# An attention-and-experts kernel: one stack moved ahead, the routing steps dealt out anew, rotary rotations in fours, and scatters that wait for TensorE once a turn

## The reference

```python
def reference(x, Wq, Wk, Wv, Wo, bo, router_w, router_bias, wg, wu, wd, swg, swu, swd):
    xn = layernorm(x)
    # attention: 16 query heads of 16, one key/value head, window of 64 keys
    q, k, v = heads(xn @ Wq), xn @ Wk, xn @ Wv
    q, k = rope(q, dims=8), rope(k, dims=8)     # x1,x2 = dims 0:4, 4:8
    scores = q @ k.T * 16**-0.5 + window_mask   # 0 <= i - j < 64
    attention = (softmax(scores) @ v).merge_heads() @ Wo + bo
    # ffn: 64 experts, top 4 of softmax(logits), chosen by logits + bias
    logits = xn @ router_w
    idx = top_k(logits + router_bias, 4)
    gates = normalised softmax(logits)[idx]
    routed = sum over the 4: gate * (silu(xn @ wg[e]) * (xn @ wu[e])) @ wd[e]
    shared = sum over 2: (silu(xn @ swg) * (xn @ swu)) @ swd
    return x + attention + routed + shared
```

## Time and profile before

| | us |
|---|---|
| median of three runs | 364.16 (363.85 to 364.17) |
| the profiled execution, its own time | 364.63 |
| its span | 363.3 |
| busy: PE, PEld | 337.3, 250.7 |
| busy: DVE, ACT, POOL | 250.7, 181.7, 251.7 |
| turns 0 to 15 | 30.4 to about 150 |

### The profile page before, as it was taken

One profiled execution on the slowest core, in us unless ns is written; L12 is line 12 of the kernel. 1 busy time (PEld: TensorE's weight loads), 2 busy tenths in 40 slices (PEclk: granted clock), 3 DMA queues, 4 the chain that ended last, 5 costly groups with the idle time before them and its releaser, 6 DMA issues.

```text
span 363.3 us, 8649 instructions
## 1 busy us (share of the span) xinstructions
PE 337.3 (93%) x2711; PEld 250.7 (69%) x2711; DVE 250.7 (69%) x721; ACT 181.7 (50%) x343; POOL 251.7 (69%) x506
## 2 busy tenths in 40 slices
PE   6978779899999999999999999999999999999982
PEld 3776546666665665589999999999975456655572
DVE  4778788988999997556456545444476376668686
ACT  2677378797688786454555555555442101110100
POOL 6467388878778777425666667778884777777774
PEclk9989899999999999999999999999999999999998
DMA  8950235645496567689988764587974344444444
GB/s 253 230 148 1 63 104 153 199 146 163 140 254 168 163 200 214 199 249 255 351 289 259 246 197 155 189 255 253 328 261 154 98 120 130 131 125 122 130 130 130
DMA packets 73036, 66.81 MB, mean 184 GB/s; under 512 B 9053, under 2 KB 68701, under 8 KB 72993
## 3 DMA queue, kind: packets, MB, share of 16 engines
q1 hardware_dynamic: 66433, 49.30, 45.8%
q0 software_dynamic: 6144, 16.79, 14.8%
q10 hardware_dynamic: 416, 0.18, 0.3%
HBM read 36.78 MB, written 29.23 MB: 182 GB/s over the span
## 4 chain that ended last, share of the span: by engine, by line
PE 70%; DVE 17%; issue 5%; ACT 5%; DMA 1%; POOL 1%; SPq 1%; DVEq 0%; POOLq 0%; ACTq 0%
PE bank L665 17%; PE bank L604 15%; PE bank L690 10%; PE bank L624 7%; PE bank L639 5%; PE bank L418 4%; DVE xall L1102 3%; PE bank L406 2%; PE bank L555 2%; PE bank L487 2%; DVE xall L1339 2%; PE bank L530 1%; ACT xall L861 1%; DVE xall L1096 1%; DMA wdn<-edges 1%
## 5 line engine op out<-in xcount | busy, mean ns | idle before, releaser
L1517 POOL DMA_INDIRECT xs_d<-spare,slot_i x64 | 63.7, 996 | 24.9 <-issue 7.3
L1609 POOL DMA_INDIRECT wall<-y_d,y_row x64 | 62.7, 980 | 24.9 <-issue 18.9
L665 PE MATMUL bank<-xall,spare 128*128 x508 | 63.8, 278 | 0.0
L1293 DVE TENSOR_TENSOR spare<-bank,spare 64x512 f32<-64x512 f32 (+1 forms) x64 | 44.1, 690 | 28.2 <-ACT spare L910 27.3
L665 PEld LDWEIGHTS bank<-xall,spare 128*128 128x128 f32 x508 | 59.4, 192 | 2.1
L1544 POOL COPY spare<-wall 128x256 f32 x127 | 49.1, 408 | 17.0 <-PE bank L665 9.1
L604 PE MATMUL bank<-xnT,xall 128*128 128x512 f32 x128 | 57.3, 594 | 0.0
L923 ACT ACTIVATE spare<-bank 128x512 f32<-128x512 f32 (+1 forms) x62 | 33.7, 593 | 28.0 <-PE bank L690 18.6
L861 ACT ACTIVATE xall<-bank 98x1024 bf16<-98x1024 bf16 x32 | 32.9, 1027 | 19.3 <-PE bank L437 17.7
L604 PEld LDWEIGHTS bank<-xnT,xall 128*128 128x128 f32 x128 | 24.1, 190 | 25.2 <-issue 24.4
L886 ACT ACTIVATE xall<-bank 128x512 f32<-128x512 f32 x16 | 9.5, 597 | 59.6 <-PE bank L604 59.6
(11 more groups left out here) (174 smaller groups left out, 635.3 us busy)
## 6 DMA issues: line engine op xcount, KB each, us to landing
y_d<-spare SPq DMA_DIRECT2D x31, 512.0 KB, 4.1
wall<-in_wg SPq DMA_DIRECT2D x16, 256.0 KB, 3.4
wall<-in_wu SPq DMA_DIRECT2D x16, 256.0 KB, 4.3
wdn<-in_wd SPq DMA_DIRECT2D x16, 256.0 KB, 4.5
spare<-xs_d SPq DMA_DIRECT2D x32, 128.0 KB, 3.5
small<-xs_d SPq DMA_DIRECT2D x32, 128.0 KB, 3.6
wall<-in_x SPq DMA_DIRECT2D x4, 512.0 KB, 5.4
base_d<-spare SPq DMA_DIRECT2D x16, 128.0 KB
```

The source lines that it names most:

```text
L665: ins = pe.matmul(up_bank_of(G)[:, j * P:(j + 1) * P], wcur[i % NW][:, c * 2 * F:(c + 1) * 2 * F], x_half[c][:, bass.ds(o, P)], start=c == ...
L1293: ins = dve.tensor_tensor(hT[G % 2][half, 0:n], up_bank_of(G)[F:P, 0:n], sg[0:F, 0:n], ALU.mult)
L1517: pool.indirect_dma_start(out=xs_d, out_offset=bass.IndirectOffsetOnAxis(ap=slot_i[:, T, k:k + 1], axis=0), in_=x_n[b][:, t, :], in_offset ...
L1609: pool.indirect_dma_start(out=yk[:, T, k, :], out_offset=None, in_=of, in_offset=bass.IndirectOffsetOnAxis(ap=y_row[:, T, k:k + 1], axis=0 ...
```

## The change

TensorE's and ScalarE's `stack(1, 1)` come ahead of the totals of the routing instead of behind them. In turn 0 VectorE does `near(1)` before the routing step instead of after it. One `yield` more splits the ranks (both halves' additions in one step) from the two steps with `max` and `slot_i`. `route_at` has four places: two as before, the third now before `place(T)`, the fourth between `place(T)` and `near(T+1)`. `cast(3, 0)` moves from ScalarE's turn 1 to the end of turn 0. `expert_row()` moves ahead of `place(T)` on TensorE. GpSimd rotates tiles 4 to 7 with four instructions on four tiles at once, between the scatters of turn 0 and of turn 1, tiles 8 to 11 with four instructions between the scatters of turn 5, and tiles 12 to 15 in turn 9; `roped` counts tiles up to 3 and then fours. One rotation buffer moves into a free part of another region, and the cosines and sines are stored twice. The scatters of a turn wait only for `maxima(T, 0)`, and `SCATTERED_AT` deals out 4 or 5 of them to each turn.

```diff
--- before.py
+++ after.py
@@ -57,7 +57,7 @@
     inv = np.exp(-np.log(np.float32(ROPE_BASE)) * (np.arange(0, 2 * ROT, 2).astype(np.float32) / np.float32(2 * ROT))).astype(np.float32)
     theta = (pos[:, None] * inv[None, :]).astype(np.float32)
     part = np.arange(P)
-    rows = lambda a: np.ascontiguousarray(a.reshape(TPB, P, ROT).transpose(1, 0, 2).reshape(P, TPB * ROT))
+    rows = lambda a: np.ascontiguousarray(np.repeat(a.reshape(TPB, P, 1, ROT), 2, 2).transpose(1, 0, 2, 3).reshape(P, TPB * 2 * ROT))
     f32 = {
         "ident": np.eye(P),
         "cos": rows(np.cos(theta)),
@@ -214,7 +214,7 @@
     wproj = ar.take(NC * NPROJ).rearrange("p (c n) -> p c n", c=NC)
     qrow = [ar.take(H * (SROWS + MROWS), bf16).rearrange("p (h n) -> p h n", h=H) for _ in range(2)]
     qtok = [r[:, :, 0:SROWS].rearrange("p h (c d) -> p h c d", d=HD) for r in qrow]
-    rope = [ar.take(H * 2 * ROT).rearrange("p (h i d) -> p h i d", h=H, i=2) for _ in range(2)]
+    rope = [r.take(TPB * H * 2 * ROT).rearrange("p (t h n) -> p t h n", t=TPB, h=H) for r in (early, ar)]
     rest = ar.take(H * HD).rearrange("p (h d) -> p h d", d=HD)
     SCORES_AT = ar.o // D
     NQ = 3
@@ -321,10 +321,12 @@
 
     FIRST = 10
 
-    ROUTE = ((1, 1, 1), (1, 0, 1))
-    route_at = lambda T: ROUTE[T] if T < len(ROUTE) else (0, 0, 2 - T % 2 if T < 12 else 1)
+    ROUTE = ((1, 1, 0, 1), (1, 1, 0, 0), (0, 0, 1, 1), (0, 0, 1, 0), (0, 0, 1, 1), (0, 0, 1, 0), (0, 0, 1, 1), (0, 0, 1, 0),
+             (0, 0, 1, 1), (0, 0, 0, 1), (0, 0, 1, 1), (0, 0, 1, 1))
+    route_at = lambda T: ROUTE[T] if T < len(ROUTE) else (0, 0, 0, 1)
     EXPERT_ROW, EXPONENTS, BIAS_AT = 13, 4, 18
-    SCATTERED_AT = lambda T: 6 if T in (NT - 4, NT - 3) else 4
+    SCATTERED_AT = lambda T: 5 if T in (2, 3, 4, 6, 7, 8) or T > 9 else 4
+    roped_with = lambda T: T + 1 if T < TPB else TPB + T // TPB
 
     NORM = ((0,), (1,), (2, 3))
 
@@ -725,13 +727,14 @@
             for t in late_tile(T, 2):
                 project(t)
             if T == 0:
+                stack(1, 1)
                 totals()
                 for i in range(2):
                     rank(i)
             if T:
                 scores(T - 1, 0, 0)
                 scores(T - 1, 0, 1)
-            if T + 1 < NT:
+            if 0 < T < NT - 1:
                 stack(T + 1, 1)
             if T > 1:
                 attention(T - 2)
@@ -740,6 +743,8 @@
                 scores(T - 1, 1, 1)
             for t in late_tile(T, 3):
                 project(t)
+            if T == EXPERT_ROW:
+                expert_row()
             place(T)
             if 0 < T < NT - 1:
                 weigh(T - 1, 0)
@@ -747,8 +752,6 @@
                 stack_k(T + 2)
             if 0 < T < NT - 1:
                 weigh(T - 1, 1)
-            if T == EXPERT_ROW:
-                expert_row()
             if 1 < T < NT - 1:
                 project_out(T - 2)
 
@@ -845,7 +848,7 @@
             if part == 0:
                 if T >= 2:
                     act.wait_ge(s["q_T"], 2 * (T - 2) + 2)
-                act.wait_ge(s["roped"], T + 1)
+                act.wait_ge(s["roped"], roped_with(T))
             else:
                 act.wait_ge(s["q_left"], 2 * T + 1)
             source = q if part == 0 else rest
@@ -965,7 +968,7 @@
         for T in range(NT):
             for t in late_tile(T, 0):
                 copy_q(t)
-            if T + 2 < NT:
+            if T + 2 < NT and T != 1:
                 cast(T + 2, 0)
             if T + 1 < NT:
                 stack(T + 1, 0)
@@ -975,6 +978,8 @@
                 cast(T + 2, 1)
             for t in late_tile(T, 2):
                 copy_q(t)
+            if T == 0:
+                stack(1, 1)
             if T:
                 scores(T - 1, 0, 0)
                 scores(T - 1, 0, 1)
@@ -985,9 +990,10 @@
                 scores(T - 1, 1, 1)
             for t in late_tile(T, 3):
                 copy_q(t)
-            if T + 1 < NT:
+            if 0 < T < NT - 1:
                 stack(T + 1, 1)
             if T == 0:
+                cast(3, 0)
                 act.wait_ge(s["c32"], 16)
                 act.activation(unread[:, :], ident[:, 0:1], ACT.Exp)
             if T == EXPONENTS:
@@ -1214,6 +1220,9 @@
                 dve.wait_ge(s["ranked"], i + 1)
                 dve.tensor_tensor(lifted[:, ts, :], bank[2 + i][:, :].rearrange("p (t e) -> p t e", e=E),
                                   starts[:, i, :].unsqueeze(1).to_broadcast([P, 8, E]), ALU.add).then_inc(s["rank_read"], 1)
+            yield
+            for i in range(2):
+                ts = slice(8 * i, 8 * i + 8)
                 dve.wait_ge(s["rank_read"], i + 1)
                 for t in range(8 * i, 8 * i + 8):
                     ins = dve.max(pos8[:, t, :], lifted[:, t, :])
@@ -1390,10 +1399,14 @@
                 next(route, None)
             if T + 2 < NT:
                 leave(T + 2, 1)
-            place(T)
             for _ in range(steps[2]):
                 next(route, None)
-            if T + 1 < NT:
+            place(T)
+            if T == 0:
+                near(1)
+            for _ in range(steps[3]):
+                next(route, None)
+            if 0 < T < NT - 1:
                 near(T + 1)
             if T:
                 output(T - 1)
@@ -1472,8 +1485,7 @@
             pool.wait_ge(s["kv_out"], b + 1)
             k = qk[:, ts, H, :]
             x1, x2 = k[:, :, 0:ROT], k[:, :, ROT:2 * ROT]
-            cs = k32["cos"].rearrange("p (t d) -> p t d", d=ROT)
-            sn = k32["sin"].rearrange("p (t d) -> p t d", d=ROT)
+            cs, sn = [k32[n].rearrange("p (t d) -> p t d", d=2 * ROT)[:, :, 0:ROT] for n in ("cos", "sin")]
             pool.tensor_tensor(krope[0], x1, cs, ALU.mult)
             pool.tensor_tensor(krope[1], x2, sn, ALU.mult)
             pool.tensor_tensor(krope[2], x1, sn, ALU.mult)
@@ -1490,21 +1502,23 @@
             prep(pool.tensor_tensor(krest[1], krest[0], parts[:, :, 1, :], ALU.subtract))
             pool.tensor_copy(parts[:, :, 2, :], krest[1]).then_inc(s["k_split"], 1)
 
-        def rotate(T):
-            t = T % TPB
-            pool.wait_ge(s["proj_q"], T + 1)
-            q = qk[:, T, 0:H, :]
-            x12 = q[:, :, 0:2 * ROT].rearrange("p h (i d) -> p h i d", i=2)
-            over = lambda v: v[:, t * ROT:(t + 1) * ROT].unsqueeze(1).unsqueeze(1).to_broadcast([P, H, 2, ROT])
-            if T:
-                pool.wait_ge(s["roped"], T)
-            pool.tensor_tensor(rope[0], x12, over(k32["cos"]), ALU.mult)
+        def rotate(lo, hi):
+            pool.wait_ge(s["proj_q"], hi)
+            q = qk[:, lo:hi, 0:H, :]
+            x12 = q[:, :, :, 0:2 * ROT]
+            n, t = hi - lo, lo % TPB
+            over = lambda v: v[:, 2 * ROT * t:2 * ROT * (t + n)].rearrange("p (t d) -> p t d", t=n).unsqueeze(2).to_broadcast([P, n, H, 2 * ROT])
+            a, b = [r[:, 0:n] for r in rope]
+            first, second = slice(0, ROT), slice(ROT, 2 * ROT)
+            if lo:
+                pool.wait_ge(s["roped"], roped_with(lo - 1))
+            pool.tensor_tensor(a, x12, over(k32["cos"]), ALU.mult)
             yield
-            prep(pool.tensor_tensor(rope[1], x12, over(k32["sin"]), ALU.mult))
+            prep(pool.tensor_tensor(b, x12, over(k32["sin"]), ALU.mult))
             yield
-            pool.tensor_tensor(x12[:, :, 0], rope[0][:, :, 0], rope[1][:, :, 1], ALU.subtract)
+            pool.tensor_tensor(x12[:, :, :, first], a[:, :, :, first], b[:, :, :, second], ALU.subtract)
             yield
-            pool.tensor_tensor(x12[:, :, 1], rope[0][:, :, 1], rope[1][:, :, 0], ALU.add).then_inc(s["roped"], 1)
+            pool.tensor_tensor(x12[:, :, :, second], a[:, :, :, second], b[:, :, :, first], ALU.add).then_inc(s["roped"], 1)
             yield
 
         def scatter():
@@ -1565,30 +1579,27 @@
                 find_down(G + 1)
 
         pool.wait_ge(s["c32"], 16)
-        def rotate_whole(T):
-            for _ in rotate(T):
+        def rotate_whole(lo, hi):
+            for _ in rotate(lo, hi):
                 pass
 
-        rotate_whole(0)
+        rotate_whole(0, 1)
         prepare_k(0)
-        rotate_whole(1)
+        rotate_whole(1, 2)
         prepare_k(1)
         prepare_k(2)
-        rotate_whole(2)
-        rotate_whole(3)
+        rotate_whole(2, 3)
+        rotate_whole(3, 4)
         prepare_k(3)
         slots = scatter()
         for T in range(NT):
 
-            pieces = rotate(T + TPB) if T < NT - TPB else iter(())
+            if T == 1:
+                rotate_whole(TPB, 2 * TPB)
+            pieces = rotate(T + 3, T + 3 + TPB) if T in (TPB + 1, 2 * TPB + 1) else iter(())
             for i in range(SCATTERED_AT(T)):
-                if T > 0:
-                    if i < 2:
-                        pool.wait_ge(s["by_query"], PER_T * T + 2 * i + 2)
-                    elif i == 2:
-                        pool.wait_ge(s["by_key"], PER_T * (T - 1) + 3)
-                    else:
```

(3 more changed lines are left out.)

## The result

The changed kernel takes 371.54 us (median of 4 runs, 370.05 to 372.79), the kernel before, run beside it, 364.17. The ratio is 1.0202, with a 95% interval of [1.0172, 1.0232]: slower by 1.7 to 2.3%. A second comparison on another occasion gives 369.45 for 364.14, ratio 1.0123 [1.0056, 1.019].

The account below looks back on a forecast made before the run. It took PE to bound the kernel (busy 93% of the span), with the change acting on turns 0 to 15. Terms +1.9, +2.0, +3.7 and -0.5 gave +7.1 on 364.63; less some for contention, it said 370.9, range 365.2 to 375.5.

Parts of the forecast that it names:

- the late rotation in turn 2: Turn 2: GpSimd rotates tiles 4 to 7 only by 54.1, so ScalarE's cast is late and the 4.3 us lead goes.
- turn 3 starts later: Start of turn 3: 61.4 against 60.52, 0.9 lost, plus 1.0 for the low clock; +1.9 us.
- steps ahead of `place`: Turns 3 to 11: routing steps moved ahead make PE wait for VectorE's `place`; +2.0 us, from -0.5 to +3.
- turns 5 and 9: Four-tile rotations between scatters end late, so ScalarE's cast is 1.45 and 2.25 us too late; +3.7 us.
- rest: Remaining turns: `expert_row` moved ahead removes PE's 0.48 us wait; -0.5 us.
- Turns 0 and 1: a gain: `near(1)` no longer stands behind the routing step; turn 1 at about 40.8, turn 2 at 48.9, 4.3 us ahead.
- Contention prolongs the steps: Alternative for the routing steps moved ahead of `place`: contention makes them longer, +3 us instead of +2.0.
- Each scatter no longer waits for TensorE gains nothing: Scatters end earlier, at about turn 13, but turns 12 to 15 run on PE; no gain by itself.
- the cheap rotations: Rival: four large rotation instructions take 2.0 us together and the clock holds in turn 3; sum +1.9, 366 us; chance 0.17.
- the faster case: Rival: the cast of tile 4 is not late, the first two turns' 4.3 us stay; -2.8, 361.4 us; chance 0.07.
- low clock more than priced: Rival: dear rotations add 2.7 us, or low clock behind turn 9's wait up to 1.7; 374 to 375 us; chance 0.16.

Follow-up runs that it names:

- 2b: Changed kernel with all three four-tile rotations ahead of the scatters of turns 0, 5 and 9; 363.0 us, 0.9949 of the kernel before (364.14).
- experiment 6: Changed kernel with four-tile rotations ahead of their turn's scatters and routing steps of turns 2 to 11 behind `place(T)`; 362.33 us, ratio 0.9957 to the kernel before.
- f3: Changed kernel, rotations ahead of the scatters of turns 0, 5 and 9, as single-tile instructions; 428.13 us, ratio 1.104 where the kernel before takes 389.55.
- second set: Four kernels (two of them the changed kernel with edits, one it unedited, one the kernel before with four-tile rotations) run where the kernel before takes 364.14 us.
- experiment 5: Kernel before with only the four-tile rotations of the change, its own waits, routing and scatters kept; 372.49 us, ratio 1.0213 to the kernel before.
- experiment 2: Changed kernel with all three four-tile rotations ahead of their turn's scatters, on a chip where the kernel before takes 391.34 us; 434.0 us, ratio 1.1143.

## Why the prediction was right, by its own steps

The time and the sign came out: 370.9 was said, 371.54 measured, and in the profiled execution +5.4 where the sum was +7.1. That the number is so near is in part luck. Against the profiled execution three terms are 1.1 to 1.2 us too high and one is 1.7 too low, and on the second occasion the same kernel took 369.45. The mechanism of the largest loss, the late rotation in turn 2, was right. The terms, against the turn starts of before and after:

| term | predicted | measured |
|---|---|---|
| turn 3 starts later | +1.9 | +0.84 |
| steps ahead of `place` (turns 3, 4, 6, 7, 8, 10, 11; the prediction has +0.2 for turn 5 in it) | +2.0 | +0.87 |
| turns 5 and 9 | +3.7 | +1.82, +3.53, together +5.35 |
| rest (turns 12 to 14, then to the end) | -0.5 | -0.92, -0.74 |

- **Turns 0 and 1: a gain, as said, and larger.** Turn 1 starts at 39.54 (40.8 said), turn 2 at 47.11 (48.9). 1.1 of it lies ahead of the turns: turn 0 starts at 29.26 instead of 30.39, as the granted clock is 1.00 from 20 to 23 where it was 0.50 from 20 to 23 before. In the second profiled execution of the changed kernel it is 0.71, 0.50 and 0.50 there and turn 0 starts at 30.00, so this differs from execution to execution and is no effect of the change. Turn 1 itself is 7.57 long (8.1 said). Which of the edits brings what in these two turns, no run takes apart.
- **Turn 2: the mechanism was right, shown by 2b, two sizes were off and cancelled.** `slot_i` was ready at 43.27, not 44.8, and the first scatter at 44.16. The four rotation instructions took 1.27, 1.26, 0.73 and 0.73, 3.96 from first start to last end, not 3.4: the slope of 1.7 ns an element read from the earlier trace rows was too low. The estimate of 3.9 from the Trainium skill (GPSIMD Engine Reference, section 3.1, Elementwise) was the better one; the trace, with 3.96, agrees with it. The cast began at 53.23 instead of 54.1, and the low clock took the 0.9 back: PE's `project`, 1.03 at full clock, took 1.91. Turn 3 starts at 61.36; the chain of waits alone was said to give 61.4, and I had added 1.0 for the low clock on top.
- **Steps ahead of place: the wait is there, its price was not.** PE waits 1.48 before line 445 in turn 4, which is 8.55 long (8.9 said), turn 7 7.60 (7.7), turn 8 7.17 (7.6), turn 10 7.43 (7.3), turn 11 7.13 (7.55). But experiment 6, which moves the steps back, gains nothing measurable. That they save at `near` what they cost at `stack_k` fits the table, where the turns of 2b other than 9 are 0.96 shorter than those of 6, but is argued. The step that failed is the +2.0 as a cost of the place of the steps.
- **Turns 5 and 9: 1.65 too small, and the mechanism wrong.** I had ScalarE's cast late by 1.45 and 2.25 in the turn behind. It starts 0.99 into turn 6 (the row names PE as releaser; the rotation ended at 86.79, 0.1 before), and the turn is 0.45 longer than said; in turn 10 it is in time, 0.3 ahead of the turn. What costs is inside turns 5 and 9: VectorE held 1.7 and 1.6 us, PE idle as long, and in turn 9 the low clock behind it. "Contention prolongs the steps" stood in the text as +3 for the wrong term; the term for the rotations held no price for VectorE beside them. That a hold of this length needs the long instruction is shown by f3.
- **Rest.** PE's wait for `expert_row` in turn 13 is gone: 6.39 for 7.24.
- **"Each scatter no longer waits for TensorE gains nothing": it does not cost here either.** 2b has one wait and is faster than the kernel before. On the other chip all kernels with one wait are slower than those with four, which does not show that the wait is the cause.

Of the rivals, the cheap rotations and the faster case are out by the 3.96; low clock more than priced did occur in turn 9, but was offset by turns 0 to 2. The best versions measured are 2b and 6, 0.5% faster than the kernel before on the second set's chip: the new order of turns 0 and 1 has gained 5.5 us at turn 3 (2b), and of that 1.1 to 1.8 is left at the end, most of the rest going in turn 9.

## What to carry to other kernels

Instructions merged to save their fixed cost must be placed by the time of their last result: four tiles' work in one group makes the first tile as late as the fourth, here 6.3 us. Price a long GpSimd instruction also by what VectorE has beside it, since its copies, casts and two-input instructions within SBUF stood here until it was over. Where a gain in one turn disappears, compare the start of every turn: the turn that gives it back is seen at once.

## What the runs showed of the hardware

- A VectorE copy, cast, `tensor_scalar` or two-input instruction that reads and writes SBUF, beside a 128x512 GpSimd instruction, was held until the other's end: 2.13, 2.72, 2.16 and 2.87 us for what takes 0.41, 0.33, 0.17 and 0.18, whatever its own length. Two GpSimd instructions back to back hold it over both (75.77 to 78.24, VectorE done at 78.44). The other way round occurs too: at 83.99 in the changed kernel line 1094 took its usual 0.30, and GpSimd's 128x256 instruction beside it, which starts at 83.93, took 0.95 instead of 0.73.
- Other VectorE instructions go on. Two of its reductions from `bank`, in PSUM, took their usual 0.87 at 81.13 beside line 1517, while the cast of 16 elements behind them, from SBUF to SBUF, took 0.45 and ended at 82.49, with GpSimd at 82.44. And eight `max` within SBUF took their usual time beside the whole of line 1515 in 2b:

```profile
42.00 1.09 DVE L1228 MAX8 wdn<-wdn 128x8 f32<-128x64 f32 x8
```

- The Trainium skill (SBUF — State Buffer, section Who interferes with whom) describes an exclusive lock of this kind, and the trace agrees as to which instructions are held and that they stand still. It gives the lock to the one that issues first. The starts in the records do not show that order: in turn 5 the held instruction starts 0.56 before the GpSimd instruction, during a scatter, and at its usual 0.41 would have ended before it; in turn 9 and in experiment 5 (49.51) it is the same. When each asks for the lock, no view shows.
- A scatter alone prolongs VectorE's work little. From 28 to 160 us of the changed kernel, 46 instructions of the lines that were held elsewhere (1094, 1102, 1117, 1119, 1230) start during a scatter with no rotation right behind it; the longest delay among them is 0.21 us (line 1094 at 107.68, 0.51 for 0.30). Whether the scatter in front lengthens a hold, no run separates.
- One and the same kernel is 0.5% faster than the kernel before on one chip and 11% slower on another (2b and 2), and the kernel before takes 364 and 391 us on them. VectorE, ScalarE and GpSimd are busy about as long on both (VectorE 252.3 us in 2b, 250.5 in experiment 2); what differs is the time in which they all stand, and signals of TensorE that arrive late, as the one at 77.11.
